# Reordering the offset stage's transfers, loading the far tables during the last batch and letting VectorE evict four lead z rows, in a deformable-convolution block

## The reference

```python
x = x + L0(gn(x))     # two 3x3 convs (16 channels each), batch norm, each scaled by a sigmoid map
                      # that a 1x1 conv and a 3x3 conv make from the branch and position planes
x = x + L1(gn(x))     # modulated deformable 3x3 convolution
# L1:
offs = conv3x3(x, offset_w) + offset_b          # 2 offsets for each of 9 taps
mask = 2 * sigmoid(conv3x3(x, mod_w) + mod_b)   # one modulation for each tap
sampled = bilinear(x at (h + ky + off_y, w + kx + off_x)) * mask
out = einsum('nckhw,ock->nohw', sampled, weight) + bias
out = relu(batchnorm(out))                      # statistics over batch and pixels
```

## Time and profile before

| what | value |
|---|---|
| time, median of 3 runs | 423.75 us (423.46 to 424.14) |
| the profiled execution's own time | 425.59 us |
| span of its trace | 423.8 us |
| PE, DVE, ACT, POOL busy, share of the span | 74%, 75%, 60%, 48% |
| mean granted TensorE clock | 0.905 of full |

### The profile page before, as it was taken

The page is one execution under the profiler, slowest core; times in us unless marked ns, Lnnn a source line. Parts: engine busy times, 40 slices in busy tenths (PEclk is TensorE's granted clock), DMA queues, the critical chain, the costliest instruction groups (busy, mean ns, idle before and its releaser), DMA issues.

```text
span 423.8 us, 14386 instructions
## 1 busy us (share of the span) xinstructions
PE 313.0 (74%) x6057; PEld 203.1 (48%) x6058; DVE 319.8 (75%) x625; ACT 252.8 (60%) x380; POOL 204.3 (48%) x242
## 2 busy tenths in 40 slices
PE   0079999848747419899989989898998999870470
PEld 0022334312213106777757777677775777760460
DVE  5456267833689852999979999799999799993266
ACT  1023322405047108888888888788888888880355
POOL 9770000199491001666646665556666466656000
PEclk9999999969679558999999999999999999996565
DMA  7799200178580643300011001001100000000005
GB/s 226 131 234 239 48 2 0 26 212 235 128 208 9 128 97 90 97 28 3 29 29 44 6 28 28 29 11 40 29 29 26 4 5 3 3 4 19 2 0 198
DMA packets 18106, 28.65 MB, mean 68 GB/s; under 512 B 6890, under 2 KB 7465, under 8 KB 18029
## 3 DMA queue, kind: packets, MB, share of 16 engines
q1 hardware_dynamic: 12397, 19.40, 17.1%
q0 software_dynamic: 2400, 5.07, 5.2%
q10 hardware_dynamic: 3246, 3.27, 3.5%
HBM read 8.03 MB, written 5.83 MB: 33 GB/s over the span
## 4 chain that ended last, share of the span: by engine, by line
PE 42%; ACT 28%; DVE 8%; DMA 7%; SPq 6%; issue 5%; ACTq 1%; POOL 1%; DVEq 1%; POOLq 0%
ACT hx L931 17%; PE ps L641 10%; PE ps L771 9%; ACT zreg L1014 8%; PE ps L584 6%; PE ps L605 5%; PE ps L654 4%; DMA hx<-xpad 3%; SPq L440 3%; PE ps L595 2%; SPq L345 2%; ACT zreg L999 2%; PE ps L780 1%; DMA x_sb<-in_x 1%; DVE x_sb L1397 1%
## 5 line engine op out<-in xcount | busy, mean ns | idle before, releaser
L561 POOL TENSOR_TENSOR prod<-prod 128x416 f32<-128x416 f32 x128 | 134.9, 1075 | 119.4 <-DVE prod L1311 119.4
L1311 DVE TENSOR_TENSOR prod<-ps,hy 128x480 f32<-128x480 f32 (+1 forms) x256 | 137.6, 600 | 23.7 <-PE ps L780 20.9
L780 PE MATMUL ps<-zreg,hx 64*64 64x96 f32 x4608 | 113.1, 247 | 0.0
L931 ACT ACTIVATE hx<-ps 128x576 f32<-128x576 f32 x131 | 78.2, 648 | 49.2 <-PE ps L771 28.5
L780 PEld LDWEIGHTS ps<-zreg,hx 64*64 64x64 f32 x4608 | 101.0, 132 | 7.5
L1018 ACT ACTIVATE hx<-hx,rbias 128x1152 f32<-128x1152 f32 x64 | 81.1, 1267 | 0.0
L1319 DVE TENSOR_REDUCE areg<-prod 128x32 f32<-128x448 f32 x128 | 72.7, 608 | 0.5 <-POOL prod L561 0.4
L641 PE MATMUL ps<-preg,sel 26*128 26x288 bf16 x260 | 42.4, 281 | 31.0 <-ACT zreg L1014 18.1
L771 PE MATMUL ps<-wzp,sreg 128*128 128x144 bf16 x512 | 43.1, 227 | 0.0
L641 PEld LDWEIGHTS ps<-preg,sel 26*128 26x128 bf16 x260 | 19.9, 91 | 46.5 <-issue 31.0
L1014 ACT ACTIVATE zreg<-ps 128x576 f32<-128x576 f32 x64 | 42.1, 658 | 0.0
(11 more groups left out here) (178 smaller groups left out, 354.9 us busy)
## 6 DMA issues: line engine op xcount, KB each, us to landing
scratch<-zreg SPq DMA_DIRECT2D x12, 240.0 KB, 4.2
sreg<-scratch SPq DMA_DIRECT2D x12, 192.0 KB, 2.5
out<-x_sb SPq DMA_DIRECT2D x8, 256.0 KB, 2.1
x_sb<-in_x SPq DMA_DIRECT2D x3, 512.0 KB, 4.9
areg<-xpad POOLq DMA_DIRECT2D x23, 66.0 KB, 3.6
areg<-xpad SPq DMA_DIRECT2D x23, 66.0 KB, 2.7
sreg<-scratch SPq DMA_DIRECT2D x4, 336.0 KB, 3.3
zreg<-xpad POOLq DMA_DIRECT2D x15, 66.0 KB, 4.1
```

The source lines that it names most:

```text
L561: pool.tensor_tensor(slots[:, :, 0:2 * moved], slots[:, :, 0:2 * moved], slots[:, :, 2 * KEPT:6 * KK], ALU.add).then_inc(folded, 1)
L780: return pe.matmul(g_ps(g, h)[u * W:(u + 1) * W, k - TAPS[h][0], :, :], hx[s, (t + u) % 4, k, :], z_sb[s, y + u + k // 3:y + u + k // 3 + ...
L931: act.activation(hx[:, t % 4, :, :].rearrange("p k (h x) -> p h k x", h=2), dist_ps(bank).rearrange("p h (k x) -> p h k x", k=KK), ACT.Abs)\
L1311: mul = vector.tensor_tensor(pv[:, n0:n1], gv, wv[:, n0:n1], ALU.mult)
```

## The change

There are four groups of edits.

In the offset stage, SP issues the rows of chunks 6 and 7 ahead of store 1. DVE makes all four of its splits at once after the second normalisation, ahead of the first offsets, where it made one ahead of each quarter's. Store 2 moves behind the regrouping of quarter 2, and load piece 0 waits for two stores and no longer for three. Of the 9 DMAs that regroup quarter 2, ACT now issues 4, between `save_parts(NQ - 2)` and its own `offsets(NQ - 1)`. Quarter 2's DMAs wait until those of quarters 0 and 1 have landed (`px_ready`). The order of the three index groups in the tile parts changes from tap, part, image to part, image, tap, so DVE writes runs of 9 elements, and the 12 source partitions of a regrouping DMA are 9 apart where they were adjacent.

In the first block, POOL issues the position planes after its rows of chunk 2 where it issued them before chunk 0.

At the end, far_tab moves to the start of the z tile. POOL clears it in four pieces between the folds of the last image's steps 6 to 9, SP loads it from there on, and ACT waits for those loads before it writes the output into the same place.

At each image's begin, DVE evicts lead rows 0 to 3 (with a semaphore `lead_low` of its own) and ACT evicts rows 4 and 5. ACT's waits on the stores move accordingly.

```diff
+        SYNC_TAPS = 5
-        far_tab = zflat[:, NPIX:NPIX + B * KW + 2 * B * P128]
+        far_tab = zflat[:, 0:B * KW + 2 * B * P128]
-            .rearrange("p (y k q b) -> p y k q b", y=HH, k=KK, q=NPART)
+            .rearrange("p (y q b k) -> p y q b k", y=HH, k=KK, q=NPART)
+        DVE_LEADS = 4
+        FAR_PIECES = 4
...
+        def regroup_offsets(eng, q0, q1, taps=range(KK)):
+
+            n = 2 * CH_ROWS * W
+            g, at = q0 // 2, q0 % 2 * n
+
+            eng.wait_ge(tp_saved, q1 + CREDIT)
+            for k in taps:
+                eng.dma_start(px[g * NXP:(g + 1) * NXP, k, at:at + (q1 - q0) * n],
+                              tpart[ds(k, NXP, step=KK), q0 * n:q1 * n]).then_inc(px_ready, 16)
...
             rows_for(0, 1, 2, 3)
             store_parts(0)
-            rows_for(4, 5)
+            rows_for(4, 5, 6, 7)
             store_parts(1)
-            rows_for(6, 7)
-            regroup_offsets(0, 2, 0)
+            regroup_offsets(sync, 0, 2)
+
+            sync.wait_ge(off_ready, NCH)
+            sync.wait_ge(xparts_stored, 16 * B * 2)
+            load_piece(0, 0)
+            sync.wait_ge(px_ready, 16 * (1 + PX_DMAS))
+            regroup_offsets(sync, 2, 3, range(0, SYNC_TAPS))
             store_parts(2)
-
-            sync.wait_ge(off_ready, NCH)
-            sync.wait_ge(xparts_stored, 16 * B * (NQ - 1))
-            load_piece(0, 0)
-            regroup_offsets(2, 3, PX_DMAS)
             store_parts(NQ - 1)
-            regroup_offsets(3, 4, 2 * PX_DMAS)
+            sync.wait_ge(px_ready, 16 * (1 + 2 * PX_DMAS))
+            regroup_offsets(sync, 3, 4)
+            sync.wait_ge(xparts_stored, 16 * B * NQ)
...
-            pool.wait_ge(attpad_zeroed, 1)
-            for dy in range(3):
-                at = dy * C + NATT
-                pool.dma_start(attrep[at:at + NPOS, 1:1 + H, :].rearrange("p r x -> p (r x)"),
-                               d["pos"][3 * dy * NPOS:(3 * dy + 1) * NPOS, :]).then_inc(pos_loaded, 16)
             for c in range(NCH):
                 pool.wait_ge(norm1, (c + 1) // 2 + 1)
                 replicate(pool, c, POOL_ROWS, xrep, xrep_last)
+                if c == 2:
+                    pool.wait_ge(attpad_zeroed, 1)
+                    for dy in range(3):
...
+                piece = i - (NT // 2 - HH // 2 + 6)
+                if 0 <= piece < FAR_PIECES:
+                    n = (B * KW + 2 * B * P128) // FAR_PIECES
+                    pool.memset(far_tab[:, piece * n:(piece + 1) * n], 0.0).then_inc(far_zeroed, 1)
+
-            pool.wait_ge(acc_ready, NT)
-            pool.memset(far_tab[:, 0:B * KW], 0.0).then_inc(far_zeroed, 1)
-            pool.memset(far_tab[:, B * KW:], 0.0).then_inc(far_zeroed, 1)
             pool.wait_ge(reach_ready, 2)
...
             save_offsets(NCH - 1)
+            save_parts(NQ - 2)
+            act.wait_ge(px_ready, 16 * (1 + PX_DMAS))
+            regroup_offsets(act, 2, 3, range(SYNC_TAPS, KK))
             offsets(NQ - 1)
-            save_parts(NQ - 2)
             save_parts(NQ - 1)
...
-                act.wait_ge(xparts_stored, 16 * B * (NQ - 1))
-                for j in range(ZLEAD):
+                for j in range(DVE_LEADS, ZLEAD):
...
-                    if t == CH_ROWS:
+                    if t == CH_ROWS - 2:
 
                         act.wait_ge(xparts_stored, 16 * B * NQ)
...
+                if c == 0:
+                    act.wait_ge(far_loaded, 16 * (B + 2))
...
             def offsets(q):
 
                 y = q * CH_ROWS
-                for step in range(4):
-                    split_rows(q, step)
...
             vector.wait_ge(norm2, NCH)
+            for q in range(NQ):
+                for step in range(4):
+                    split_rows(q, step)
...
+            def lead_rows(b):
+
+                for j in range(DVE_LEADS):
+                    vector.wait_ge(lead_made, b * ZLEAD + (j + 1))
+                    vector.tensor_copy(z_sb[:, j, :], z_ps(j % 2, LEAD_BANKS[j])).then_inc(lead_low, 1)
+
+            lead_rows(0)
             for i in range(NT // 2):
                 weigh(i, 0)
                 weigh(i, 1)
+                if (i + 1) % (HH // 2) == 0 and i + 1 < NT // 2:
+                    lead_rows((i + 1) // (HH // 2))
```

27 lines of the change are left out of this document (12 added, 15 removed).

## The result

The changed kernel takes 421.96 us (median of 20 runs, 416.18 to 423.71), the kernel before beside it 424.24 us (422.71 to 429.05). The ratio is 0.990, 95% interval 0.9873 to 0.9927; it compares only the executions that were not in a slower state (15 of the changed kernel's 20), so it is not the quotient of the two medians. So the kernel is faster, as forecast, but by 2.3 us between the medians (about 4 us by the ratio) and not by 14.3: 421.96 lies far outside the range of 406.5 to 415.5.

A forecast was written before the change was run, and what follows sets the result against it. Most of the chain lies in the unchanged main loop; gains were sought in the offset stage, image begins and end. 2.6 + 6.6 + 0.5 + 4.6 = 14.3 us, from 423.75 to 409.5 us; own range 407.5 to 412, overall 406.5 to 415.5.

The forecast's parts named there:

- Rows 6 and 7 ahead of store 1: Offset stage: SP's rows issued earlier, chunk 6 at the high clock, first regrouping 2.6 us earlier (bounds 0.4 to 3.4).
- rival of late rows: Offset stage: chunk 7 still late and at the low clock, gain 0.4; with slow issue 413.4 us, chance 0.15.
- slow issue: Second half of that rival: ACT's and SP's DMAs, issued at once, take 1.2 us each, 1.7 us lost.
- VectorE's splits: Offset stage: DVE's early splits fit into its idle 12.94 us and cost nothing on the paths to the loop.
- DVE's splits in POOL's way: Rival, offset stage: splits beside POOL's work delay chunk 4, priced at 2 us, total 411.5 us, chance 0.08.
- the forecast's own signs of being wrong: Convolutions of chunks 3 to 5 later, ACT's four DMAs over 4 us, or regrouping DMAs over 1 us each.
- First block: Start of the kernel: moving the position planes' three DMAs taken at nothing, from -0.7 to +0.7 us.
- From the first regrouping to the loop: Offset stage's end: 28.1 us becomes 21.5, limited by the table of far tiles; gain 6.6 us (bounds 2.7 to 7.2).
- Lead rows: Image begins: 0.15 us at each of three, 0.5 us in all; bounds a gain of 1.0 or loss of 1.2.
- End: Behind the last fold: far z rows start at about 387.5, not 392.08; gain 4.6 us (bounds 3.9 to 4.9).

The follow-up runs named there:

- after: The trace of the changed kernel, all edits on the kernel before: median 421.96 us, ratio 0.990; this profiled execution took 422.39 us.

## Why the prediction was wrong

**Rows 6 and 7 ahead of store 1: the step that failed.** The first half held: SP's rows of chunk 6 in 3.06 us (3.2 forecast), chunk 6 behind a gap of 1.16 us (under 2) at the high clock. Then "with 2.5 us for the landing PE starts at about 127.8". That is 19.1 us behind chunk 4's start; it was 19.9, since POOL's rows took up to 5.2 us to land beside store 1, and not 2.5. Worse, chunk 7 was priced at the high clock after that wait; behind 5.71 us of idling it took 5.18 us, 2.4 more. The two make up the whole difference between -2.6 and +0.6. The forecast's own row should have warned: it had read that the clock fell a little over 2 us behind PE's last work, and it left PE without work for about 4 us ahead of chunk 7. The rival of late rows had this price (4.53 us) at a chance of 0.15; its other half, slow issue, did not come (ACT's four DMAs took 0.8 us each, not 1.2). The bounds held this case (128.3 and 4.53) only with chunk 4 where it was. And chunk 4 came 2.2 us later. In the kernel before POOL's late rows had been covered by SP's rows, which took 6.00 us to issue: PE started chunk 7 at 130.39 without a wait. The forecast should have counted POOL's list from chunk 4's end, as it counted SP's, with the landing of a transfer that has a store beside it. Moving POOL's rows ahead of its split brought the first regrouping 7.1 us earlier and the time to 413.35 us.

**VectorE's splits: taken at nothing, measured 2.2 us; a rival had them.** "DVE's splits in POOL's way" gave 2 us at chunk 4 and a chance of 0.08; chunk 4 lost 2.2, and putting the splits back returned 2.5. That the size fits is in part luck: the rival had POOL lose some 4 us, and POOL was 0.7 to 1.5 us late. It was also the first of the forecast's own signs of being wrong, a convolution of chunks 3 to 5 that starts later. The main text had called the splits covered because DVE idles there. That looked at the engine that does the work, not at what it does to the others: a cast of DVE's third split takes 1.65 us beside POOL's split where it takes 0.49 alone, and POOL's subtraction 1.8 where it takes 1.4. The Trainium skill (SBUF — State Buffer, SBUF: two separate sides) names the shared port; the trace agrees in kind. How POOL's delay reached SP's rows of chunk 4, by store 0, which waits for POOL's first split, or by the transfers' own rate, was not separated.

**First block: 0 ± 0.7, measured +2.3.** The step "moving them frees nothing on POOL" was right and beside the point. While the planes are loaded, all transfers are slow, for some 8 us. With the planes in front that lay in a time when PE had nothing to do, up to 18 us; behind chunk 2 it hits rows that PE waits for. Chunk 0, landing 5 us earlier, only moved PE's wait behind it, and chunk 1 then took 4.99 us instead of 3.26.

**From the first regrouping to the loop: right.** 6.1 us instead of 6.6, with the path, the limit (table, then copies) as named; the landing took 8.6 us (9.0 forecast), ACT's four DMAs 3.3 (3.1). From the end of the copies to PE it was 0.7 us and not 0.1, for the reason given below at the lead rows.

**The loop's start: a cost that was in no term, 3.7 us between these two traces.** The forecast took the steps of the loop as they were. In the changed kernel PE enters the loop at a granted clock of 0.50 and has one or two slow steps (13.47, 12.11, 13.46 and 11.29 us for the first three in after, its repeat, with the planes in front and with the splits back; 9.73 before). But with the old stretch it varies too: 11.85 and 11.45 us with the far tables alone and the lead rows alone. In the fifteen traces with the new stretch and without fillers it is 11.1 to 13.8, 12.4 on average, against 11.0 in the three with the old one. So about 1.4 us is an estimate of what the change costs here, from few traces, and the rest of the 3.7 is one fast start in the trace of before. When exactly the clock rises differs between executions, and nothing here tells what decides it.

**Lead rows: 0 instead of 0.5.** The forecast had ACT's two rows done earlier than DVE's copies. But PE makes rows 4 and 5 only when DVE has evicted rows 0 and 1; so DVE's four copies end at 220.7, ACT's two rows come last, at 220.9, and PE goes on as late as before.

**End: right.** 4.8 us to the z rows (4.6 forecast, bound 4.9). The 1.1 us behind them is about what executions with the same end differ by (30.6 to 31.6 us from the z rows on with the new end, 30.9 to 31.7 with the old).

Summed up: of 14.3 us, 10.9 came at the two places that were worked out along a chain (regrouping, end), and 8.8 were lost where engines off that chain, or the clock, came in (2.3 + 2.2 + 0.6 + 3.7, of the last some 2 by chance, if the estimate above holds); 1.1 came unasked and not shown to be the change's. The range was too narrow because the lost terms were held at zero or better, though the earlier trace rows and two of the rivals already named what could be lost in the offset stage.

## What to carry to other kernels

When a queue is freed of its late item, work out the next-latest item of every other queue that feeds the same wait, with its own landing; the cover it had was the thing that was removed. Price matmuls behind a wait of several microseconds at the low clock: here 24 of them took 4.5 to 5.4 us behind waits of 3.9 to 6.6 us, and 2.78 behind waits of 1.2 to 1.6 us. Where a loop starts at the low clock, read its first steps from several traces before a difference is put down to a change. And a load beside which all transfers slow down belongs where nobody waits, even if it then delays the very first rows.

## What the runs showed of the hardware

- The three loads of the position planes (4 partitions with 16.9 KB each, 66 KB a load) are followed by some 8 us in which the core's transfers move 76 to 178 GB/s in place of 216 to 302, with the DMA engines' share at 0.9 to 1.3. It came in each of the four places behind chunk 0's rows; in front of the list it is 118 to 154 GB/s from 14 to 18 us. Whether the few partitions, the long rows or the source does it was not tried.
- Filler matmuls (26 partitions deep, 0.36 us each) kept PE busy from 144 to 160 us; the granted clock fell from 1.00 to 0.50 between 144 and 146 us and stayed there while they ran.
- The granted clock at the loop's start rose at times that differ by up to 10 us between executions of nearly the same program: between 162 and 164 us in the kernel before, near 170 with the far tables alone, near 166 with the lead rows alone, near 172 in the changed kernel.
- In the last quarter DVE writes a bf16 part of 288 elements in 0.30 us, and the subtraction takes 0.46, in the new order of the tile parts, where the strided writes before took 0.80 and 1.43; the forecast had taken this at nothing, and it was on no critical path.
